# Loading the output-projection weights during attention, with shallower staging buffers in the projections

## The reference

```python
qk = (x @ Wqk_w.T + Wqk_b).reshape(b, n, H, E, 2)      # H = 8 heads, E = 64
q, k = qk[..., 0], qk[..., 1];  v = x @ Wv_w.T + Wv_b
attn = softmax(q k^T) / sqrt(512)
x = layernorm(x + (attn v) @ Wo_w.T + Wo_b)
# feed-forward: a dense 4096 x 4096 layer, and 8 rank-16 adapters weighted by a top-2 router
x = layernorm(x + x @ W_base.T + b_base + lora(x))
```

## Time and profile before

| | us |
|---|---|
| three timed runs: median, lowest, highest | 4126.47, 4102.93, 4306.67 |
| the profiled execution | 4120.75 |
| span of its slowest core, first to last instruction | 4119.0 |
| spans of the 8 cores | 4041.4 to 4119.0 |
| PE busy | 3190.7 (77%) |
| DVE, ACT, POOL busy | 1362.7, 827.0, 714.7 |
| moved by DMA | 444.75 MB |

### The profile page before, as it was taken

The page is one execution under the profiler, slowest core; times in us unless marked ns, Lnnn a source line. Parts: engine busy times, 40 slices in busy tenths (PEclk is TensorE's granted clock), DMA queues, the critical chain, the costliest instruction groups (busy, mean ns, idle before and its releaser), DMA issues.

```text
span 4119.0 us, 46186 instructions; the slowest of 8 cores (4041.4 to 4119.0 us)
## 1 busy us (share of the span) xinstructions
PE 3190.7 (77%) x13476; PEld 1202.4 (29%) x13476; DVE 1362.7 (33%) x1908; ACT 827.0 (20%) x1412; POOL 714.7 (17%) x567
## 2 busy tenths in 40 slices
PE   3777697778788888888788947652899997999960
PEld 2655243322222222121122212110344442444420
DVE  0000000035666656566565417771100002111123
ACT  1222000003333334333333412320000000000000
POOL 2111100000000000000000013353222212444425
PEclk9899799876777767676666659986899998999975
DMA  8999544410000000000000033315454535666648
GB/s 235 284 275 269 171 134 145 159 46 1 1 1 3 1 1 1 3 1 1 3 1 1 1 115 108 108 57 179 129 162 143 162 109 190 200 206 205 214 106 190
DMA packets 450638, 444.75 MB, mean 108 GB/s; under 512 B 21472, under 2 KB 402529, under 8 KB 450402
## 3 DMA queue, kind: packets, MB, share of 16 engines
q1 hardware_dynamic: 347490, 341.12, 28.0%
q10 hardware_dynamic: 102912, 100.68, 7.9%
HBM read 340.01 MB, written 100.66 MB: 107 GB/s over the span
## 4 chain that ended last, share of the span: by engine, by line
PE 55%; DVE 9%; issue 6%; DMA 5%; POOL 2%; DVEq 0%; ACT 0%; SPq 0%; POOLq 0%; ACTq 0%
PE pf L155 24%; PE sS L155 10%; PE rb L155 9%; PE a L155 7%; DVE racc L557 4%; DMA outT<-outst 2%; DVE x2g L983 2%; POOL tmpf L973 2%; PE po L155 2%; DMA wstgo<-woT 1%; PE sS L582 1%; PE pss L155 1%; PE psq L155 1%; PE pstS L155 1%; DVE rrec L736 1%
## 5 line engine op out<-in xcount | busy, mean ns | idle before, releaser
L557 DVE TENSOR_REDUCE racc<-sS 128x1 f32<-128x512 f32 x1024 | 681.6, 689 | 1250.6 <-PE sS L155 1238.9
L155 PE MATMUL pf<-x2h,wqf 128*128 128x512 bf16 x4096 | 909.9, 380 | 5.9 <-DVE hs L1319 5.9
L703 ACT ACTIVATE probs<-rb 128x512 bf16<-128x512 f32 x1024 | 542.4, 598 | 914.8 <-PE rb L155 912.0
L155 PE MATMUL sS<-kT,qT 64*128 64x512 bf16 x1024 | 472.6, 479 | 153.3 <-DVE racc L557 115.5
L155 PEld LDWEIGHTS pf<-x2h,wqf 128*128 128x128 bf16 x4096 | 396.8, 98 | 505.8 <-issue 39.7
L155 PE MATMUL a<-probs,V 128*65 128x512 bf16 x1024 | 378.2, 497 | 0.0
L155 PE MATMUL pk<-xbf,wk_bf 128*128 128x256 bf16 x2048 | 270.3, 294 | 138.6 <-ACT xbf L333 64.2
L1344 POOL CAST wqf<-wstgf 128x1024 bf16<-128x1024 f32 x256 | 265.0, 1042 | 601.1 <-DMA wstgf<-wbT 432.4
L1410 DVE SCALAR_TENSOR_TENSOR res2c<-pf,bB_sb,x2h 128x1024 bf16<-128x1024 f32 x64 | 82.2, 1284 | 865.3 <-PE pss L155 793.3
L155 PE MATMUL rb<-qT,kT 64*128 64x512 bf16 x1024 | 340.0, 480 | 0.3 <-PE rb L155 0.2
L844 POOL CAST wo_bf<-wstgo 128x1024 bf16<-128x1024 f32 x16 | 16.6, 1042 | 1704.3 <-DMA wstgo<-woT 1704.3
(11 more groups left out here) (104 smaller groups left out, 1708.8 us busy)
## 6 DMA issues: line engine op xcount, KB each, us to landing
wstgf<-wbT SPq DMA_DIRECT2D x256, 512.0 KB
xstg<-xrot SPq DMA_DIRECT2D x128, 512.0 KB
xscr<-xbf ACTq DMA_DIRECT2D x128, 256.0 KB, 5.5
xvb<-xscr SPq DMA_DIRECT2D x128, 256.0 KB, 2.6
outT<-outst ACTq DMA_DIRECT2D x64, 512.0 KB, 5.2
xqb<-xscr SPq DMA_DIRECT2D x32, 512.0 KB, 3.2
xq<-xscr SPq DMA_DIRECT2D x32, 512.0 KB, 3.5
x2scr<-x2g ACTq DMA_DIRECT2D x32, 512.0 KB, 2.8
```

The costliest lines, as they stand in the source:

```text
L155: return lambda e: e.matmul(o, l, r, start=st, stop=sp, skip_group_check=True)
L557: e.reduce_max(d, srd, AX.X, negate=True),
L703: e.activation(d, srd, AF.Exp),
```

## The change

1. The 16 loads of `woT` and their 16 casts move from the start of the O stage to the start of the attention stage. `wo_bf` (32 KB per partition) is now held from the start of the kernel to the end of the O stage.
2. `wload` loads as many chunks at once as its staging buffer holds, and the staging buffers of K, V and Q have half the size: 16 loads of 2 chunks (512 KB) instead of 8 of 4, and 16 casts of 128 x 1024.
3. In the K stage there are 3 buffers `xstg` instead of 4 and 2 buffers `xbf` instead of 4, used in turn through the whole stage.
4. In the V stage the buffer index becomes a count modulo 3, though 4 buffers `xvb` are still held.
5. `bv_sb` is loaded and cast at the start of the V stage.
6. The loads of `x2h` use streams `ld` and `sc` in turn.

```diff
     def wload(dst_bf, dstR_list, src_dram, stg, stgR, n_chunks, cw):
-        for g in range(n_chunks // 4):
+        per = stg[0].shape[1] // cw
+        for g in range(n_chunks // per):
...
-                    wstg = [sbP("wstg%d" % i, [128, 2048], F32) for i in range(2)]
+                    wstg = [sbP("wstg%d" % i, [128, 1024], F32) for i in range(2)]
...
-                    xstg = [sbP("xstg%d" % i, [128, 1024], F32) for i in range(4)]
-                    xbf = [sbP("xbf%d" % i, [128, 1024], BF16) for i in range(4)]
+                    xstg = [sbP("xstg%d" % i, [128, 1024], F32) for i in range(3)]
+                    xbf = [sbP("xbf%d" % i, [128, 1024], BF16) for i in range(2)]
...
-                                bi = g % 4
+                                bi = (kg * 8 + g) % 3
+                                bj = (kg * 8 + g) % 2
...
-                                              waits=[tl] + xbfR[bi].wr())
+                                              waits=[tl] + xbfR[bj].wr())
...
+                    t_bvl = s.op("SP", lambda e: e.dma_start(bv_sb[:],
+                                                             c_bv.ap()),
+                                 dma="ld")
...
-                            dma="sc")
+                            dma=("sc" if g % 2 else "ld"))
```

More of the change, by code:

```diff
@@ L208, in wload @@
             tc = s.op("POOL",
-                      lambda e, d=dst_bf[:, 4 * g * cw:(4 * g + 4) * cw],
-                      srd=stg[st_i][:, 0:4 * cw]: e.tensor_copy(d, srd),
+                      lambda e, d=dst_bf[:, per * g * cw:(per * g + per) * cw],
+                      srd=stg[st_i][:, 0:per * cw]: e.tensor_copy(d, srd),
                       waits=[tl])
             stgR[st_i].did_read(tc)
-            for j in range(4):
-                dstR_list[4 * g + j].did_write(tc)
+            for j in range(per):
+                dstR_list[per * g + j].did_write(tc)
     with ExitStack() as st0:
@@ L286, in build_program @@
             OTtmpr = [Res() for _ in range(4)]
+            wo_bf = sbA("wo_bf", [128, 4 * D], BF16)
+            woR = [[Res() for _ in range(4)] for _ in range(4)]
             with ExitStack() as stI:
@@ L298, in build_program @@
                                          kc=32, h=8)[:, :, :, 64:65]
-                t = s.op("POOL", lambda e: e.memset(vones, 1.0), waits=[t_bv])
+                t = s.op("POOL", lambda e: e.memset(vones, 1.0),
+                         waits=consts_fence)
                 for r in Vr:
@@ L385, in build_program @@
                     sbP = lambda n, sh, dt: stP.enter_context(nc.sbuf_tensor(n, sh, dt))
+                    bv_sb = sbP("bv_sb", [1, 512], F32)
+                    bvbf = sbP("bvbf", [1, 512], BF16)
+                    t_bvl = s.op("SP", lambda e: e.dma_start(bv_sb[:],
+                                                             c_bv.ap()),
+                                 dma="ld")
+                    t_bv = s.op("POOL", lambda e: e.tensor_copy(bvbf[:],
+                                                                bv_sb[:]),
+                                waits=[t_bvl])
                     wv_bf = sbP("wv_bf", [128, 32 * 512], BF16)
                     wvR = [Res() for _ in range(32)]
-                    wstg = [sbP("wstgv%d" % i, [128, 2048], F32) for i in range(2)]
+                    wstg = [sbP("wstgv%d" % i, [128, 1024], F32) for i in range(2)]
                     wstgR = [Res(), Res()]
@@ L448, in build_program @@
                     wqR = [Res() for _ in range(32)]
-                    wstg = [sbP("wstgq%d" % i, [128, 2048], F32) for i in range(2)]
+                    wstg = [sbP("wstgq%d" % i, [128, 1024], F32) for i in range(2)]
                     wstgR = [Res(), Res()]
@@ L506, in build_program @@
                     sbP = lambda n, sh, dt: stP.enter_context(nc.sbuf_tensor(n, sh, dt))
+                    wstgo = [sbP("wstgo%d" % i, [128, 1024], F32)
+                             for i in range(2)]
+                    wstgoR = [Res(), Res()]
                     probs = sbP("probs", [128, 8192], BF16)
@@ L522, in build_program @@
                     rbcR = [Res(), Res()]
+                    for hh in range(4):
+                        for c in range(4):
+                            st_i = c % 2
+                            src_ = woT.ap()[c * 128:(c + 1) * 128,
+                                            hh * 1024:(hh + 1) * 1024]
+                            tl = s.op("SP", lambda e, d=wstgo[st_i], src=src_:
+                                      e.dma_start(d[:], src),
+                                      waits=wstgoR[st_i].wr(), dma="ld")
+                            wstgoR[st_i].did_write(tl)
+                            tc = s.op("POOL",
+                                      lambda e,
+                                      d=wo_bf[:, c * D + hh * 1024:
+                                              c * D + hh * 1024 + 1024],
+                                      srd=wstgo[st_i][:]: e.tensor_copy(d, srd),
+                                      waits=[tl])
+                            wstgoR[st_i].did_read(tc)
+                            woR[c][hh].did_write(tc)
                     with nc.psum_tensor("sS", [128, 1024], F32) as Sg, \
@@ L811, in build_program @@
                 sbP = lambda n, sh, dt: stP.enter_context(nc.sbuf_tensor(n, sh, dt))
[L812 to L815, removed]
                 xq = sbP("xq2", [128, 32 * 512], BF16)
@@ L829, in build_program @@
                 tmpfR = [Res(), Res()]
[L831 to L847, removed]
                 with nc.psum_tensor("po0", [128, 512], F32) as po0, \
```

38 lines of the change are left out of this document (18 added, 20 removed).

## The result

The changed kernel is slower: the ratio to the kernel before is 1.0181, 95% interval 1.0123 to 1.0239, which on 4120 us is about 75 us. The medians of ten executions each, 4207.36 us of the changed kernel and 4203.55 of the one before, include executions in which the four cores of one die ran at a lower granted clock, and the ratio leaves those out. The profiled execution took 4197.3 us, with a span of 4195.3 on core 1, the slowest.

What follows compares the result with a forecast made beforehand. K was taken as bound by DMA, V by PE, the O opening by SP's wo loads ahead of xq. Terms -45 + 30 + 20 + 3 + 0 = +8 on 4120.75 gave 4129 us; range 4074 to 4188.

Steps and rivals of the forecast that it cites:

- The likeliest case: Whole kernel: no measurable change, 4129 us, with the K stage and weight openings near the middle of their bounds; chance 0.52.
- rival C: K stage: writes' landing does not shrink, x loads fill what writes leave, cast stands openly; +75 us, total 4184; chance 0.20.
- the K stage's "+20": K stage with fewer x buffers: landings shrink with the bytes in flight, 15 us per stage, +20 with irregular landings.
- Rival B: K stage keeps 2.81 us per tile as its engines stay full; halved loads cost 0 to +11; 4076 to 4087 us; chance 0.22.
- The price of +75: K stage upper bound: landing, cast and hand-over make 6.8 us a pair, 64 x 1.17 = +75 us.
- The O opening: Start of the O stage: wo loads and casts go, xq is issued earlier; -45 us, bounds -42 to -48.
- The openings: Weight loads ahead of K, V and Q, halved to 512 KB: +30 us in all, between +22 and +39.
- The other estimate: Weight openings of K, V and Q: fixed cost of about 2 us per transfer, 8 us per stage, 24 in all.
- wo under attention: Start of attention: wo loads and POOL's casts end near 917, 17 us before the first mrow transfer; cost 0.
- Rival D: Start of attention: prefetch outlasts its cover, each us beyond adds one; chance 0.06 together with anything unseen.
- The V stage: V stage, index modulo 3 into four xvb buffers: loads barely fit; +3 us, bounds 0 to +15.
- bv and x2h: bv load ahead of the V weights: 0; x2h loads on two semaphore groups: 0, bounds -5 to +3 us.

## Why the prediction was wrong

**The result**, 4195 us by the ratio and 4197.3 in the profiled execution, lies above my range (4188 us). The likeliest case was no measurable change; what came is 1.8% slower, which stays short of the 2% bound, with an interval that reaches over it. It is rival C, to which I gave 0.20, nearly with its price: K +75 forecast, +80.5 measured. Of its mechanism one half was right, the cast that stands openly between two writes. The other half, that the x loads fill what the writes leave, was not: the share fell to 0.79.

**The step that failed** is the K stage's "+20": "a landing that shrinks alike is 4.7 us, where 4.46 is needed". I worked with the mean of the bytes under way, 15% fewer, and let each landing shrink by as much. But a landing depends on what is sent with it. With two copies, writes and loads are released by the same casts and leave together; the mean falls because the queues stand empty between bursts, not because a burst is smaller. The median landing stayed at 5.5 us at share 0.79, and with half-size loads, so with less in the burst, it was 4.1 us. My upper bound, landing + cast + hand-over = 6.8 us a pair, was the answer, and 6.9 was measured (median of the cores; 7.04 on the slowest). Two copies alone gave the loss (454.4), the third copy took it away (370.6, and 364.2 in the changed kernel). The 0.96 share, my argument against C, said that the engines were busy with the buffers of then, not that they would stay so. Nor did it say that they were full: four writes brought 21 us out of the same stage.

**Rival B's mechanism** was a queue that always has something left. The Trainium skill ("DMA: Bandwidth & Descriptors", section on queues, rings and completion order) has engines taking turns between queues that have work; the trace neither confirms nor denies the turns. What B needed, a transfer always at work, is what the trace denies: in 251 to 252 almost nothing moved (0.01).

**The price of +75** came near partly by luck. As written its terms, 5.5 + 1.04 + 0.13, give 6.67 us and +67; 6.8 counts the hand-over of 0.13 twice. Measured, the hand-over is 0.48 (0.37 before the cast, 0.11 behind it) and the mean landing 5.36, the median of the cores: 5.36 + 1.05 + 0.48 = 6.89. A hand-over that I had too short and a landing that I had slightly too long offset each other. The third load buffer's loss, +6 alone, did not appear with three copies (364.2), and what it adds with two is not isolated.

**The O opening**, -45 forecast: -47.0, and -46.6 to -48.1 in all seven kernels with early wo loads. Right in its mechanism, that everything behind the wo loads moves up. What comes late next is not the xq tile, for which I left 6.8 us: DVE starts 4.3 us after xq's issue, released by PE.

**The openings**, +30 in all: +26.2, and +27 alone. The size was right, since wo's own loads, through two buffers of the same size, were a fair row to take it from. The other estimate, 24 us from a fixed cost of each of the 8 more loads, came near as well, but not for its reason: with the same 16 loads and a third buffer the openings cost nothing.

**wo under attention**, 0: right. The loads were issued by 1027.2, 25 us ahead of the first mrow transfer (17 forecast), and attention's medians agree to 0.2 us. Rival D fell with that.

**The V stage**, +3: +1.0. PE waited 0.7 us in all for xvb (core 1, 556 to 813):

```profile
PE pv L155 <- DMA xvb<-xscr: 0.7, 2, 0.5
```

The "at most 0.4 us for each of 128 tiles" would have been 51 us, which doesn't fit the bound of +15 beside it; neither came near. **bv and x2h**, 0: from the first issue of x2h to DVE's copy of the router's output the first half takes 28.4 to 35.5 us on the cores, before 28.5 to 36.8, and the ratio of the x2h edit alone is 0.9993.

With the K term at its measured size the sum is -47 + 26.2 + 80.5 + 1 = +60.7, thus 4181 us. The ratio's interval, +51 to +98 us, contains it. What is left to the 4197.3 of the profiled execution is the choice of the core that sets the time: on the slowest core of after the K stage took 459.8 us and attention 1495, 10 above the median stage and 17 above before's core 4, less 9 in the second half of the feed-forward (706 against 715): 18 us, where 16 are missing.

## What to carry to other kernels

Before a staging buffer is given up, ask which event frees it and what else the same event releases. Here one cast freed the load buffer and let the write go; two copies put load and write in step, and the queues ran dry between bursts, while one spare copy kept them apart. A high DMA share doesn't say that buffers are to spare, since it was made with them. When you estimate the loss, hold the landing time as it is, and take the hand-overs from the trace: landing, hand-over and cast add up to the measured period. Memory that a prefetch only needs later can serve the stages before it: that turned +1.8% into -1.1%.

## What the runs showed that was not expected

- The price of copies is a step: 373, 371 and 450 us for four, three and two.
- A limit was hidden behind a share of 0.96: with four writes under way instead of two the landing rose from 5.5 to between 7.4 and 8.2 us, and the stage still became 21 us shorter, at share 1.01.
- Loads of 512 KB through three buffers ran at 246 to 261 GB/s, through two at 175 to 207; 1 MB through two gave the same openings as the three small ones.
- The feed-forward's second half has two lengths, about 686 and 712 us, by pairs of cores and from execution to execution (in 11 of 28 pairs with the x2h edit and 5 of 24 without it).
